# A decoder block of 32 sequences on one core: weights and hidden activations rounded by conversion to 8-bit integers, a second tile for decayed scores, all orders rewritten

## The reference, cut to what matters

```
amax = max(|xb|)                       # over 32 values
scale = exp2(floor(log2(amax)) - 6)
q = clip(round(xb / scale), -128, 127) * scale
```

## Time and profile before

| | |
|---|---|
| runs, us | 1327.1, 1330.46, 1327.14 (median 1327.14) |
| profiled execution: own time, span | 1328.37, 1326.6 |
| mean granted TensorE clock | 0.98 |
| PE, PEld busy | 94%, 60% |
| DVE busy | 85% |
| ACT busy | 60% |
| POOL busy | 50% |
| DMA | 28.4% of 16 engines, mean 73 GB/s |

### The profile page before, as it was taken

The page is one execution under the profiler, slowest core; times in us unless marked ns, Lnnn a source line. Parts: engine busy times, 40 slices in busy tenths (PEclk is TensorE's granted clock), DMA queues, the critical chain, the costliest instruction groups (busy, mean ns, idle before and its releaser), DMA issues.

```text
span 1326.6 us, 34598 instructions
## 1 busy us (share of the span) xinstructions
PE 1242.1 (94%) x13319; PEld 796.5 (60%) x13352; DVE 1129.6 (85%) x1960; ACT 800.1 (60%) x1565; POOL 656.8 (50%) x700
## 2 busy tenths in 40 slices
PE   4778999999999999999999999999999999999864
PEld 4655556666656666666566666665666666556421
DVE  7889888888888888888888888888888889889885
ACT  3334567566666766666667666666666665666541
POOL 6767345654544445445444454454444553444332
PEclk9889999999999999999999999999999999999987
DMA  7655332222232222222222222223312222221222
GB/s 244 167 134 139 84 77 52 57 59 56 73 71 72 50 49 59 64 68 72 72 72 48 54 55 64 69 71 72 72 40 54 61 72 64 60 75 35 64 54 52
DMA packets 137331, 97.09 MB, mean 73 GB/s; under 512 B 108112, under 2 KB 110160, under 8 KB 136400
## 3 DMA queue, kind: packets, MB, share of 16 engines
q1 hardware_dynamic: 137168, 94.87, 28.4%
HBM read 37.16 MB, written 8.39 MB: 34 GB/s over the span
## 4 chain that ended last, share of the span: by engine, by line
PE 78%; DVE 7%; issue 4%; POOL 3%; ACT 3%; DMA 3%; SPq 1%; POOLq 0%; ACTq 0%; DVEq 0%
PE bank_b L549 15%; PE bank_a L549 8%; PE bank_y L603 7%; PE bank_y L667 7%; PE bank_a L539 7%; PE rt L618 5%; PE rt L568 4%; PE rt L631 4%; PE bank_o L637 4%; PE bank_b L658 4%; PE bank_a L658 4%; PE bank_o L595 2%; PE bank_y L587 2%; PE bank_y L582 1%; PE bank_o L649 1%
## 5 line engine op out<-in xcount | busy, mean ns | idle before, releaser
L3011 POOL TENSOR_TENSOR gmem<-gmem,unit_g 128x1024 bf16<-128x1024 bf16 x64 | 126.0, 1970 | 245.0 <-DVE unit_g L1512 245.0
L1459 DVE TENSOR_REDUCE negm<-rt 128x16 f32<-128x2048 f32 x64 | 146.3, 2285 | 5.4 <-PE rt L618 2.6
L2433 ACT ACTIVATE pT<-rt 128x2048 f32<-128x2048 f32 x64 | 120.1, 1876 | 26.2 <-PE rt L631 20.4
L549 PE MATMUL bank_a<-mix_r,w_Wr 128*128 128x128 f32 x1024 | 124.5, 281 | 0.9 <-POOL mix_r L2970 0.9
L667 PE MATMUL bank_y<-w2q,gmem 128*128 128x512 bf16 x479 | 113.7, 388 | 12.1 <-DMA gmem<-gmem 9.7
L549 PEld LDWEIGHTS bank_a<-mix_r,w_Wr 128*128 128x128 f32 x1024 | 119.9, 196 | 7.8 <-issue 7.7
L603 PE MATMUL bank_y<-w_Wo,yT 128*128 128x512 f32 x256 | 117.8, 603 | 4.0 <-issue 2.5
L549 PEld LDWEIGHTS bank_b<-mix_k,w_Wk 128*128 128x128 f32 x1024 | 118.5, 193 | 4.4 <-issue 3.5
L549 PE MATMUL bank_b<-mix_k,w_Wk 128*128 128x128 f32 x1024 | 119.8, 275 | 0.7 <-DMA w_Wk<-Wk 0.7
L549 PE MATMUL bank_b<-mix_g,w_Wg 128*128 128x128 f32 x1024 | 120.3, 276 | 0.0
L549 PEld LDWEIGHTS bank_b<-mix_g,w_Wg 128*128 128x128 f32 x1024 | 116.9, 192 | 2.7 <-issue 1.8
(11 more groups left out here) (186 smaller groups left out, 2765.9 us busy)
## 6 DMA issues: line engine op xcount, KB each, us to landing
qx<-qdense SPq DMA_DIRECT2D x64, 224.0 KB, 3.0
context<-ctx SPq DMA_DIRECT2D x32, 384.0 KB, 3.2
gmem<-w SPq DMA_DIRECT2D x16, 512.0 KB, 4.2
xin<-x SPq DMA_DIRECT2D x32, 256.0 KB, 3.4
out<-x SPq DMA_DIRECT2D x32, 256.0 KB, 3.1
vp<-vz SPq DMA_DIRECT2D x32, 128.0 KB, 3.1
odense<-oT SPq DMA_DIRECT2D x128, 32.0 KB, 1.9
pT<-Wv SPq DMA_DIRECT2D x1, 1024.0 KB, 8.5
```

Source lines behind the costliest of these rows:

```text
L549: done = e.matmul(bank[:, m * T:(m + 1) * T], wt[f"W{name}"][:, c, m * P:(m + 1) * P], mix[name][:, c, :], start=(c == 0), stop=(c == KT - 1))
L1459: e.tensor_reduce(negm[:, 0:H].rearrange("p (g a j) -> p g j a", g=4, a=2)[:, :, 2 * i:2 * i + 2, :], rt[:, :].rearrange("p (g j a s) -> p ...
L2433: e.activation(pT[:, :, :].rearrange("p g n -> p (g n)"), rt[:, :], ACT.Exp, scale=float(D) ** -0.5).then_inc(sem(f"act_ex{i}"), 1)
L3011: e.tensor_tensor(blocks(half), blocks(half), per_block(unit[f"g{i}"], 32), ALU.mult).then_inc(sem(f"pool_gsc{i}"), 1)
```

## The change

**Rounding of the weights.** `block_floor` now also takes five steps off the exponent bits (`TO_INT`), so that the scaled value is an integer's size. `w12_quantise` loses its rounding instruction. In its place ScalarE gets a step `w12_rounded`, a copy from f32 into an 8-bit integer tile laid over the start of the same buffer, and the last DVE instruction becomes a plain multiply of that integer tile.

**Rounding of the hidden input.** `hidden_scale` writes 8-bit integers (over `hw`), `hidden_round` is gone, `hidden_quantised` is a plain multiply. The gelu's rounding stays as it was.

**Sums turned in full.** `oden` is 128 x 128, of which 32 rows are filled, and `turn_sums` is a transpose over all rows and columns.

**Half 1 of the decayed scores apart.** `decayed(n, 1)` writes into the memory of `pT`. It no longer waits for `values_r(n, 0)`, but it must not overtake `values_x(n-2, 1)`, and `weights_x(n-2, 0)` must not overtake `values_r(n-1, 1)`.

**Orders.** All five lists are laid out anew. The loops cover n = 14 to 25 on PE, the other four engines have only lists. At the start, SP issues `x(0)` first, then columns, heads, masks, `x(1)`, and only then the weight pieces; DVE begins with `stats_q(0)`, `rates`, `halves`, `distances(0)`, `norm_mv q 0`. In PE's loop, `turn_sums` and `turn_queries` come ahead of `up(n-4,2)`, both `values_r(n-1, .)` stand together after `project k`, and `values_x(n-2,1)` stands ahead of `scores_r(n,0)`. Waits that another wait implied are left out.

```
+TO_INT = 5 * 0x0080
...
-        oden = sb("oden", [H, T])
+        oden = sb("oden", [P, T])
...
+        h_int = hw[:, 0:C // 4].bitcast(I8)
...
+        w_int = [w[:, 0:FF // 8].bitcast(I8) for w in wst]
...
+        atts = [att[:, :, :, :, :],
+                wv_rows[:, 0:24 * HALF].rearrange("p (g m k t) -> p g m k t", g=4, m=2, k=3)]
...
-                e.transpose(bank_o[:, 0:H], oden[:, :], ident[0:H, 0:H]).then_inc(sem("pe_dT"), 1)
+                e.transpose(bank_o[:, 0:P], oden[:, :], ident[:, :]).then_inc(sem("pe_dT"), 1)
...
             def decayed(n, i):
                 e.wait_ge(sem(f"pe_Rs{i}"), n + 1)
-                if i == 1:
-                    e.wait_ge(sem("pe_Ry0"), n + 1)
-                elif n:
-                    e.wait_ge(sem("pe_Ry1"), n)
+                if n:
+                    e.wait_ge(sem(f"pe_Ry{i}"), n)
...
-                e.tensor_tensor(att[:, :, :, :, :].rearrange("p g m k t -> p g (m k t)"),
+                e.tensor_tensor(atts[i].rearrange("p g m k t -> p g (m k t)"),
...
-            def block_floor(key, name, n):
+            def block_floor(key, name, n, steps):
                 e.wait_ge(sem(name), n)
-                e.tensor_scalar(upper(amax[key][:, :]), upper(amax[key][:, :]), LEAST_HALF, None,
-                                ALU.max).then_inc(sem(name), 1)
+                e.tensor_scalar(upper(amax[key][:, :]), upper(amax[key][:, :]), LEAST_HALF + steps, steps,
+                                ALU.max, ALU.subtract).then_inc(sem(name), 1)
...
-                e.tensor_tensor(blocks(h_bf), blocks(h_bf), per_block(unit["h"], 16),
+                e.tensor_tensor(blocks(h_int), blocks(h_bf), per_block(unit["h"], 16),
                                 ALU.mult).then_inc(sem("dve_hchain"), 1)
...
-            def hidden_round(n):
-                e.wait_ge(sem("dve_hchain"), 7 * n + 6)
-                e.tensor_scalar(h_bf.bitcast(FP16), h_bf, TOP, MAGIC16, ALU.min,
-                                ALU.add).then_inc(sem("dve_hchain"), 1)
...
-                e.scalar_tensor_tensor(blocks(h_bf), blocks(h_bf.bitcast(FP16)), MAGIC16,
-                                       per_block(pow2["h"], 16), ALU.subtract, ALU.mult).then_inc(sem("dve_hq"), 1)
+                e.tensor_tensor(blocks(h_bf), blocks(h_int), per_block(pow2["h"], 16),
+                                ALU.mult).then_inc(sem("dve_hq"), 1)
...
             def w12_quantise(n):
-                key, w = f"w{n % 2}", wst[n % 2]
-                e.wait_ge(sem("pool_w_scale"), n + 1)
-                e.tensor_scalar(w, w, TOP, MAGIC32, ALU.min, ALU.add).then_inc(sem("dve_w_round"), 1)
-                e.wait_ge(sem("dve_w_round"), n + 1)
+                key = f"w{n % 2}"
+                e.wait_ge(sem("act_w_int"), n + 1)
...
-                e.scalar_tensor_tensor(blocks(wq[n % 2]), blocks(w), MAGIC32, per_block(pow2[key], 32),
-                                       ALU.subtract, ALU.mult).then_inc(sem("dve_w_q"), 1)
+                e.tensor_tensor(blocks(wq[n % 2]), blocks(w_int[n % 2]), per_block(pow2[key], 32),
+                                ALU.mult).then_inc(sem("dve_w_q"), 1)
...
+            def w12_rounded(n):
+                e.wait_ge(sem("pool_w_scale"), n + 1)
+                e.activation(w_int[n % 2], wst[n % 2], ACT.Copy).then_inc(sem("act_w_int"), 1)
```

More of the change, by code:

```diff
@@ L1724, in _ @@
             first_sum(2)
+            norm_mv("q", 4)
             stats_x(2)
@@ new lines, in _ @@
+            gelu_quantised(8, 0)
+            differences(12)
+            maxima(10, 1)
+            up_out(8, 2, bank_a)
+            normalise_o(9)
+            mixed(12, "k")
+            residual(7)
+            maxima(10, 0)
+            stats_f(9)
+            gate(11)
+            norm_mv("f", 9)
+            e.wait_ge(sem("pe_Xo1"), 10)
+            decayed(11, 1)
+            stats_g(9)
+            norm_mv("g", 9)
+            weighted(9)
+            hidden(9)
+            hidden_max(9)
@@ new lines, in _ @@
+            maxima(12, 1)
+            residual(9)
+            stats_f(11)
+            maxima(12, 0)
+            mixed(14, "k")
+            gate(13)
+            gelu_quantised(10, 0)
+            norm_mv("f", 11)
+            e.wait_ge(sem("pe_Xo1"), 12)
+            decayed(13, 1)
+            stats_g(11)
+            norm_mv("g", 11)
+            weighted(11)
+            hidden(11)
+            hidden_max(11)
+            mixed(14, "v")
+            hidden_pow2(11)
+            hidden_scale(11)
@@ new lines, in _ @@
+            mixed(16, "k")
+            maxima(14, 0)
+            stats_f(13)
+            gelu_quantised(12, 0)
+            residual(11)
+            gate(15)
+            norm_mv("f", 13)
+            e.wait_ge(sem("pe_Xo1"), 14)
+            decayed(15, 1)
+            stats_g(13)
+            norm_mv("g", 13)
+            weighted(13)
+            hidden(13)
+            mixed(16, "v")
+            hidden_max(13)
+            hidden_pow2(13)
+            hidden_scale(13)
+            hidden_quantised(13)
@@ new lines, in _ @@
+            up_out(17, 2, bank_a)
+            differences(21)
+            normalise_o(18)
+            maxima(19, 1)
+            mixed(21, "k")
+            maxima(19, 0)
+            stats_f(18)
+            residual(16)
+            gate(20)
+            norm_mv("f", 18)
+            e.wait_ge(sem("pe_Xo1"), 19)
+            decayed(20, 1)
+            stats_g(18)
+            gelu_quantised(17, 0)
+            norm_mv("g", 18)
+            mixed(21, "v")
+            weighted(18)
+            hidden(18)
@@ new lines, in _ @@
+            maxima(21, 1)
+            mixed(23, "k")
+            maxima(21, 0)
+            stats_f(20)
+            residual(18)
+            gelu_quantised(19, 0)
+            norm_mv("f", 20)
+            gate(22)
+            e.wait_ge(sem("pe_Xo1"), 21)
+            decayed(22, 1)
+            stats_g(20)
+            norm_mv("g", 20)
+            mixed(23, "v")
+            weighted(20)
+            hidden(20)
+            hidden_max(20)
+            hidden_pow2(20)
+            hidden_scale(20)
@@ new lines, in _ @@
+            denominators(23)
+            second_out(21)
+            maxima(24, 1)
+            mixed(26, "k")
+            normalise_o(23)
+            residual(21)
+            up_out(22, 2, bank_a)
+            maxima(24, 0)
+            mixed(26, "v")
+            stats_f(23)
+            norm_mv("f", 23)
+            gate(25)
+            e.wait_ge(sem("pe_Xo1"), 24)
+            decayed(25, 1)
+            stats_g(23)
+            norm_mv("g", 23)
+            weighted(23)
+            hidden(23)
```

3718 lines of the change are left out of this document (2894 added, 824 removed).

## The result

The changed kernel takes 1311.2 us in the median of its four runs (1308.61 to 1312.27), the kernel before 1327.56 us beside it; the ratio is 0.9871, with a 95% interval of 0.9854 to 0.9888. That is 17 us less (15 to 19), where 18 were predicted. The profiled execution took 1312.03 us with a span of 1310.2, against 1328.37 and 1326.6 before.

A forecast was written before the change was run, and what follows sets the result against it. PE alone was taken to bound each loop pass, VectorE to be fullest in the filling. Filling -15, passes -1.5 and end -1.5 made -18 us: 1310.4 from the profiled 1328.37, predicted as 1309 us, range 1299 to 1323.

The forecast's parts named there:

- Rounding off VectorE: Filling part: the weights' rounding instruction goes from VectorE, 12.6 us less work there.
- The multiply: Filling part: 16 subtract-and-multiply instructions become plain 8-bit multiplies, 1.56 to 1.22 us each, 5.4 us less (0 to 11.0).
- Three quarters passed on: Filling part: of 20 us less on VectorE, three quarters shorten the run, -15 us (-6 to -22).
- Rival 2: Filling part: weights' work off the path and start hidden, PE limited by first sequences' chain; 1327 within 4 us; chance 0.08.
- ScalarE's copy: Filling part: 16 copies of weights to 8 bits on ScalarE, 1.03 us each, 16.5 us (9.3 to 23.6).
- Rival 1: Filling part: the weight-buffer ring, with ScalarE's copy, sets the time, not VectorE's load; 1318 us (1315 to 1323); chance 0.20.
- Start: Start: x(0), its statistics and distances come first, saving 2 us on VectorE; first PE instruction near 11 instead of 16.1 us.
- A pass: PE's loop: fewer tile-shape changes give about -0.1 us (-0.1 to +0.2) times some 18 passes, -1.5 us.
- Half 1 apart: Decayed scores in PE's loop: the removed wait gains nothing, but gives freedom to put both `values_r` late.
- Hidden rounding: VectorE's hidden rounding, 0.29 us per sequence, goes: nothing in the loop, 0.3 us plus a handover at the end.
- End: Draining the pipeline: shorter chain to the last up product and new order, -1.5 us (+2 to -4).
- Rival 3: Every pass: new ScalarE and VectorE lists delay turned maxima and stall PE before `scores_x`; 1338 at 1.3 us a pass; chance 0.10.

The follow-up runs named there:

- e1: The changed kernel with the weights rounded on VectorE as before and no ScalarE copy; 1324.4 us, ratio 0.9978.
- e2: The changed kernel with the weights' last multiply on VectorE done twice; 1335.11 us, ratio 1.0057.
- e4: The kernel before, in its own orders, with only the weights' rounding changed to the 8-bit conversion on ScalarE; 1326.32 us, ratio 0.9992.
- e12: The kernel before with 8-bit weights alone, plus four VectorE steps moved so ScalarE's conversion lies beside other VectorE work; 1327.91 us, ratio 0.9997.
- e13: The kernel before with the changed start (SyncE and VectorE) and the 8-bit weights, other orders as before; 1327.05 us, ratio 0.9988.
- e3: The changed kernel with ScalarE's conversion of each weight piece preceded by the same conversion into a spare tile; 1318.05 us, ratio 0.9922.
- e11: The kernel before with the changed start alone (SyncE and VectorE); 1326.77 us, ratio 0.9991.
- e10: The changed kernel with half 1 of the decayed scores written into half 0's tile again, with the wait this needs; 1395.32 us, single run.
- e5: The kernel before, in its own orders, with 8-bit weights, 8-bit hidden input and sums turned in full; 1325.12 us, ratio 0.9987.

## Why the prediction came out, point by point

That the sum fits is in part luck. The filling was booked 5.7 us too high; the passes and the end together were booked 4.0 us too low, and that made up for most of it.

- *Rounding off VectorE, -12.6.* Of its own work 16 x 0.68 = 10.9 us went. Right in kind; with the conversion on ScalarE in its place, 11 to 14 us come back in the new orders.
- *The multiply, -5.4.* Wrong. The step that failed is "at the most it stays where it is, 24.9 / 16 = 1.56 us" read as the price of the work, with 1.22 us set against it. The work was 1.22 us in both kernels, and 24.9 us became 24.0.
- *Three quarters passed on, -15.* The term measured -9.3. In the new orders the end moves by as much as VectorE's own work or more (`e1`, `e2`), in the old ones almost not at all (`e4`: 0.6 us at `project k(10)`, `e12`, `e13`). Rival 2, the weights' work off the path, fell with `e1`. The prediction took the share from the old trace's busy time and applied it to the edit, apart from the orders. By the profiles the orders with the old rounding of the weights are 2.0 us slower at `project k(10)` (`e1`: 401.40 against 399.37), and the 8-bit weights in them give 11.4.
- *ScalarE's copy, 1.03 us each, 16.5 in sum.* 1.054 and 16.9. Rival 1 needed VectorE to wait for it: 1.3 us in all, and doubling the copy moves the first up product by 1.9 us and the time by 6.8 (`e3`).
- *Start, -2, first PE instruction near 11.* 11.85, and 2.3 us by the profile of `e11` (1.2 by its times, whose interval includes zero).
- *A pass, -0.1.* -0.35 in a usual pass, -0.25 in the mean. The parts of the rows were nearly right (0.09 + 0.07 for the sums, 0.1 for the two `values_r`, measured 1.61 - 1.48 = 0.13, and 0.06 at `turn_x` that was left out); the "one change more, +0.1" does not exist: `project_out` takes 3.52 us against 3.53 and `scores_r` 1.08 against 1.07.
- *Half 1 apart, nothing.* As a removed wait it is nothing. What the step said besides, that it gives the freedom to put both `values_r` late, is all its worth: without it the new orders cost 83 us more (`e10`, 1395.32 against 1312.03, one run).
- *Hidden rounding, nothing in the loop.* No worth shows: `e5` has it and its pass is explained by the sums, and from `project k(31)` to the last matmul `e5` takes 117.64 us and `e4` without it 117.38.
- *End, -1.5.* -3.0 from `project k(26)` on, within the term's bounds (+2 to -4). From there to the last matmul the kernels in the old orders take 312.1 to 313.9 us and the changed one 310.6, so its size is known to about 1 us. Which of the lists gives it was not tried; the wait of the last up product stayed, 10.9 us against the 10.18 of the earlier trace rows.
- *Rival 3.* PE waits for `qx<-negT` 1.6 us in two places of the whole span. The half microsecond of room held.

The four kernels around the weights make a square (the new orders come with the other edits of the change): old orders and old rounding 1, old orders with 8-bit weights 0.9992, new orders with old rounding 0.9978, both 0.9871. What is not settled is which pieces of the new lists let VectorE's saving through. Covering the hop does not by itself, nor does the earlier start of VectorE; GpSimd's, ScalarE's and PE's lists for the first three sequences were not tried by themselves.

## What to carry to other kernels

Take the price of an instruction from its shortest, not from its mean, and ask what the rest of the mean is: here the waiting for GpSimd that sat in the old instruction was found again in its successor. Whether time freed on a full engine reaches the end depends on the orders too; here the arithmetic edit of the weights alone was worth 0.1% (not clear of nothing), the new orders with the other edits 0.2%, and all together 1.3%. Count changes of tile shape over the whole neighbourhood, as islands of strips, and give two halves that should run back to back their own tiles.

## What the runs showed of the hardware

- VectorE's multiply by a factor per block of 32 takes 1.21 us for 1024 columns of 8-bit integers; from 32-bit floats, with a subtraction in the same instruction, 1.224.
- A VectorE instruction of 32 two-byte columns (0.19 us alone) took up to 1.31 us while GpSimd was in a long instruction, and GpSimd's 1.90 us scaling up to 3.34 behind VectorE's 1.75.
- ScalarE converts 128 x 1024 floats to 8-bit integers in 1.04 to 1.06 us in all 16 cases, also beside the long instructions of VectorE and GpSimd.
- After 2 us without a matmul, in a loop in which PE had been busy, the granted clock was 0.51 for the next 3.5 us (`e10`, behind the stall that ends at 663.44). Behind the next stall of the same length, from 704.90, it stayed at 1.00.
